# Row halves and paired chunks in one attention loop, moved pieces of work in another

## The reference

```python
xn = _ln(x, lnx_g, lnx_b)                                  # first layer
yn = _ln(y, lny_g, lny_b)                                  # y: the context
q = jnp.einsum('bsc,hcd->bhsd', xn, wq)
k = jnp.einsum('btc,hcd->bhtd', yn, wk)
v = jnp.einsum('btc,hcd->bhtd', yn, wv)
a = jax.nn.softmax(jnp.einsum('bhsd,bhtd->bhst', q, k) * D ** (-0.5), axis=-1)
o = jnp.einsum('bhst,bhtd->bhsd', a, v)
```

## Time and profile before

| | |
|---|---|
| median of 3 runs | 628.16 us (627.39 to 629.56) |
| profiled execution | 629.66 us, span 627.8 us |
| mean granted PE clock | 0.98 of 2.4 GHz |
| first loop, first scores of images 0 to 3 and last scores | 115.9, 140.71, 165.45, 189.98; 304.3 us |
| second loop, the same | 411.06, 441.28, 463.97, 486.66; 589.0 us |
| busy share of the span | PE 90%, DVE 71%, POOL 61%, ACT 59% |

### The profile page before, as it was taken

The page is one execution under the profiler, slowest core; times in us unless marked ns, Lnnn a source line. Parts: engine busy times, 40 slices in busy tenths (PEclk is TensorE's granted clock), DMA queues, the critical chain, the costliest instruction groups (busy, mean ns, idle before and its releaser), DMA issues.

```text
span 627.8 us, 18969 instructions
## 1 busy us (share of the span) xinstructions
PE 566.9 (90%) x8256; PEld 416.1 (66%) x8256; DVE 444.7 (71%) x698; ACT 372.0 (59%) x623; POOL 380.6 (61%) x271
## 2 busy tenths in 40 slices
PE   9788898899999999999888979977889889889897
PEld 4566775566767767666777556664667767778765
DVE  3876728697887887786356774776888988986543
ACT  2335674657657667566462417474677777777552
POOL 1572451488989889864630231175999999977500
PEclk9789999999999999999999999997999999999998
DMA  5830015002101101010013000412422432330000
GB/s 169 238 133 2 3 40 180 2 1 42 34 7 41 26 15 40 3 40 3 2 60 123 2 0 3 99 39 64 103 67 45 96 78 52 78 77 4 2 1 15
DMA packets 33838, 31.81 MB, mean 51 GB/s; under 512 B 27124, under 2 KB 27380, under 8 KB 33756
## 3 DMA queue, kind: packets, MB, share of 16 engines
q1 hardware_dynamic: 33756, 30.60, 18.8%
HBM read 13.06 MB, written 0.23 MB: 21 GB/s over the span
## 4 chain that ended last, share of the span: by engine, by line
PE 62%; DVE 18%; ACT 8%; issue 7%; POOL 3%; DMA 1%; DVEq 0%; POOLq 0%; ACTq 0%
PE psum L1143 9%; DVE scratch L1306 6%; PE psum L1067 5%; PE psum L1119 5%; PE psum L1503 4%; PE psum L1112 4%; PE psum L1114 4%; PE psum L1526 4%; DVE scratch L1291 4%; PE psum L217 3%; POOL scratch L1291 2%; ACT scratch L1276 2%; POOL scratch L652 1%; PE psum L1073 1%; PE psum L248 1%
## 5 line engine op out<-in xcount | busy, mean ns | idle before, releaser
L1291 POOL TENSOR_TENSOR scratch<-scratch 125x896 bf16<-125x896 f32 x143 | 242.7, 1715 | 80.4 <-ACT scratch L1276 79.9
L1306 DVE TENSOR_REDUCE scratch<-psum 128x1 f32<-128x500 f32 x336 | 210.3, 672 | 23.1 <-PE psum L1067 9.6
L1276 ACT ACTIVATE scratch<-psum 125x896 f32<-125x896 f32 x192 | 173.6, 917 | 82.8 <-PE psum L1143 51.1
L1112 PE MATMUL psum<-tok_high,scratch 125*128 125x65 bf16 x1344 | 107.0, 194 | 3.3 <-issue 2.7
L1114 PE MATMUL psum<-tok,scratch 125*128 125x64 bf16 x1344 | 106.4, 194 | 0.0
L1112 PEld LDWEIGHTS psum<-tok_high,scratch 125*128 125x128 bf16 x1344 | 94.8, 98 | 13.9 <-ACT scratch L1276 6.0
L1114 PEld LDWEIGHTS psum<-tok,scratch 125*128 125x128 bf16 x1344 | 88.6, 98 | 17.1 <-issue 0.5
L1143 PE MATMUL psum<-scratch 65*128 65x448 bf16 (+1 forms) x384 | 87.3, 352 | 0.0
L1291 DVE TENSOR_TENSOR scratch<-scratch 125x896 bf16<-125x896 f32 x49 | 67.5, 1383 | 22.8 <-ACT scratch L1276 21.1
L1119 PE MATMUL psum<-tok_high,scratch 125*128 125x65 bf16 x1344 | 72.7, 194 | 4.8 <-POOL scratch L1291 3.1
L1503 PE MATMUL psum<-scratch 128*128 128x500 bf16 x168 | 64.2, 382 | 10.8 <-DVE scratch L1306 6.5
(11 more groups left out here) (340 smaller groups left out, 870.5 us busy)
## 6 DMA issues: line engine op xcount, KB each, us to landing
nrm<-scratch SPq DMA_DIRECT2D x64, 96.0 KB, 2.2
nrm<-w_third SPq DMA_DIRECT2D x32, 96.0 KB, 2.2
raw<-ctx_dram SPq DMA_DIRECT2D x4, 672.0 KB
w_third<-fifth_dram SPq DMA_DIRECT2D x3, 595.0 KB, 6.0
w_third<-third_dram SPq DMA_DIRECT2D x2, 844.0 KB, 8.9
w_third<-third_dram SPq DMA_DIRECT2D x2, 843.5 KB, 6.8
w_fourth<-fourth_dram SPq DMA_DIRECT2D x3, 542.5 KB, 5.8
scratch<-scratch SPq DMA_DIRECT2D x8, 192.0 KB, 2.6
```

Of the source, the lines that this page charges most:

```text
L1112: nc.tensor.matmul(psum[:, sums, 65 * r:65 * r + 65], rows, t1[:, c, :], start=(c == 0 and r == 0), stop=False, skip_group_check=True)
L1276: nc.scalar.activation(CR["p"][0:CP, n % RING, :].rearrange("p (f n) -> p f n", f=2), psum[0:CP, S:S + 2, 0:HALF], ACT.Exp).then_inc(self. ...
L1291: ops.tensor_tensor(CR["pl"][0:CP, n % RING, :], CR["p"][0:CP, n % RING, :], p_high(n % RING), ALU.subtract).then_inc(done, 1)
L1306: nc.vector.tensor_reduce(mxp[:, r, t:t + 1], bank(B, TB), X_AXIS, ALU.max).then_inc(self.aux_freed, 1)
```

## The change

First loop. The scores of an even chunk and of the next are issued together: the four `ya` matmuls of both, then the four `yb` matmuls. `yb` and `qb` now keep one copy on each 64-row half of the array: a row of ones or shifts first, then 63 rows. This takes away the row for feature 0: since normalized tokens sum to zero over their features, the weights of feature 0 are subtracted from all others once (`fold_keys_pool`). The `yb` matmul of column half 0 runs on rows 0 to 63, that of half 1 on rows 64 to 127. Ones are set in four places, `yb` is copied in twice (63 rows each), the two shift units cover 448 columns each, and ACT's shift copy waits for DVE's low queries, which write the same row earlier. M units move to chunks 3 to 9, O to chunk 6, N between the maxima of chunk 3.

Second loop. M units are at new places, DVE's low parts in chunks 3 and 4 (were 1 and 2; in the first image they stay), key units in chunks 0 and 1 of the first image and 9 and 10 of every image (were 0 to 2, and 8 to 10), the masked queries in chunk 5 (was 10). The tokens' casts move from POOL to ACT in chunk 2, and POOL's low tokens to chunk 3, for images 3 to 7. The first copy for `pv` (`high_act`) of image 1 moves two steps down. Image 2's transpose is issued ahead of image 1's grouping.

```diff
@@ ONES moves up; new:
+        def fold_keys_pool(pool):
+            keys = par("a2_wk").rearrange("p (h d) -> p h d", d=65)
+            nc.gpsimd.tensor_copy(keys[:, :, 64:65], keys[:, :, 0:1]).then_inc(key_scaled, 1)
+            pool.wait_ge(key_scaled, 2)
+            nc.gpsimd.tensor_tensor(keys[:, :, 0:64], keys[:, :, 0:64], keys[:, :, 64:65].to_broadcast([128, HEADS, CD]),
+                                    ALU.subtract).then_inc(key_scaled, 1)
+            pool.wait_ge(key_scaled, 3)
@@ y_ones_set
-                nc.gpsimd.memset(CR["yb", i][64:65, :], 1.0).then_inc(y_ones, 1)
+                for k in range(2):
+                    nc.gpsimd.memset(CR["yb", i][64 * k:64 * k + 1, :].bitcast(F32), ONES).then_inc(y_ones, 1)
@@ placement
-                for c in range(4, 11):
-                    at[c] += [[u] for u in FRONT[3 * c - 10:3 * c - 7]]
+                for c in range(3, 10):
+                    at[c] += [[u] for u in FRONT[3 * c - 7:3 * c - 4]]
...
-                at[3] += [[], [("N", 0)]]
-                at[5] += [[("O", 0)]]
+                at[3] += [[] for _ in range(1 - len(at[3]))]
+                at[3].insert(1, [("N", 0)])
+                at[6].insert(0, [("O", 0)])
@@ Cross.scores_pe
-                for lhs, rhs, rows in ((CR["ya", i], CR["qa", i], 128), (CR["yb", i], CR["qb", i], 65)):
-                    if c == 0 and rows != 128:
-                        self.wait_freed(pe, self.index("A", 1, b))
-                        pe.wait_ge(self.yb_in, 16 * (b + 1))
+                if n % 2:
+                    return
...
+                for m in (n, n + 1):
+                    if m >= 2:
+                        pe.wait_ge(self.probs, m - 1)
+                    for f in range(2):
+                        nc.tensor.matmul(bank(2 + 2 * (m % 2) + f, HALF), CR["ya", i][:, chunk(m)],
+                                         CR["qa", i][:, HALF * f:HALF * f + HALF], start=True, stop=False,
+                                         skip_group_check=True)
+                if n % CHUNKS == 0:
+                    self.wait_freed(pe, self.index("A", 1, b))
+                    pe.wait_ge(self.yb_in, 32 * (b + 1))
+                    pe.wait_ge(self.front_low, 2)
+                for m in (n, n + 1):
+                    for f in range(2):
+                        rows = slice(64 * f, 64 * f + 64)
+                        mm = nc.tensor.matmul(bank(2 + 2 * (m % 2) + f, HALF), CR["yb", i][rows, chunk(m)],
+                                              CR["qb", i][rows, HALF * f:HALF * f + HALF], start=False, stop=True,
+                                              skip_group_check=True)
+                        if f:
+                            mm.then_inc(self.scores, 1)
@@ copy_act, shift row
+                    if b and self is cross1:
+                        self.wait_freed(act, self.index("Q", 1, b))
+                    lo, hi = HALF * k, HALF * k + HALF
@@ Cross.turn_tokens
-                sp.dma_start(CR["yb", b % 2][0:64, :], CR["ya", b % 2][64:128, :]).then_inc(self.yb_in, 16)
+                if b:
+                    sp.wait_ge(self.yb_in, 32 * b)
+                for k in range(2):
+                    sp.dma_start(CR["yb", b % 2][64 * k + 1:64 * k + 64, :], CR["ya", b % 2][65:128, :]
+                                 ).then_inc(self.yb_in, 16)
@@ new: tokens' casts on ACT
+            def high_tokens(self, act, b, k):
+                at = slice(CHUNKS * b + 6 * k, CHUNKS * b + 6 * k + 6)
+                act.wait_ge(self.pv_done, CHUNKS * (b - 2))
...
+                nc.scalar.activation(tok[b % TOKENS][:, 6 * k:6 * k + 6, 64:128], self.src[:, at, :], ACT.Copy
+                                     ).then_inc(self.tok_high, 1)
@@ KeyCross: maxima per chunk, key units, low parts, POOL
-                    for c, n in enumerate((2, 1, 1, 2, 3, 3, 3, 2, 2, 1, 1) if b else (0, 0, 0, 0, 3, 3, 3, 3, 3, 3, 3)):
+                    for c, n in enumerate((2, 1, 3, 1, 0, 2, 3, 3, 3, 2, 1) if b else (0, 0, 1, 3, 3, 3, 3, 2, 2, 2, 2)):
...
-                    if b == 0 and c < 3:
-                        lots += [[], [], [("K", c)]]
+                    if b == 0 and c < 2:
+                        lots += [[("K", 0)], [("K", 1)]] if c == 0 else [[("K", 2)]]
...
-                    if b < BATCH - 2 and 8 <= c < 11:
-                        lots += [[]] * (2 - len(lots)) + [[("K", c - 8)]]
+                    if b < BATCH - 2 and c in (9, 10):
+                        lots += [[]] * (2 - len(lots)) + ([[("K", 0)]] if c == 9 else [[("K", 1)], [("K", 2)]])
...
+            def tokens_pool(self, pool, b, c):
+                if b == 0 and c in (1, 2):
+                    self.split_tokens(pool, 2, c - 1)
+                if b and c == 3:
+                    for k in range(2):
+                        self.low_tokens(pool, b + 2, k)
...
             def beside_act(self, act, b, c):
+                if b and c == 2 and b < BATCH - 2:
+                    for k in range(2):
+                        self.high_tokens(act, b + 2, k)
...
             def beside_dve(self, dve, b, c):
-                if c == 10 and b < BATCH - 2:
+                if c == 5 and b < BATCH - 2:
                     self.plain_dve(dve, b + 2)
@@ the sync queue in the second loop
             for b in range(BATCH):
+                if b == 1:
+                    cross2.turn_tokens(sp, 2)
                 cross2.group_keys(sp, b)
-                if 0 < b < BATCH - 1:
+                if 1 < b < BATCH - 1:
                     cross2.turn_tokens(sp, b + 1)
```

More of the change, by code:

```diff
@@ L1071, in pe_unit @@
                         pe.wait_ge(self.max_set, b + 1)
-                    for r in range(4 * k, min(4 * k + 4, ROWT)):
-                        mm = nc.tensor.matmul(psum[:, B, 128 * (r % 4):128 * (r % 4) + 128],
-                                              nmx[:, r:r + 1].to_broadcast([128, 128]), ident16[:, :],
-                                              start=True, stop=True)
+                    for r in range(3 * k, 3 * k + 4):
+                        lo, hi = max(128 * r, HALF * k), min(128 * r + 128, HALF * k + HALF)
+                        mm = nc.tensor.matmul(psum[:, B, lo - HALF * k:hi - HALF * k],
+                                              nmx[:, r:r + 1].to_broadcast([128, 128]),
+                                              ident16[:, lo - 128 * r:hi - 128 * r], start=True, stop=True)
                 elif kind == "N":
@@ L1133, in scores_pe @@
             def scores_pe(self, pe, n):
-                b, c, i = n // CHUNKS, n % CHUNKS, n // CHUNKS % 2
-                S = 2 + 2 * (n % 2)
-                for lhs, rhs, rows in ((CR["ya", i], CR["qa", i], 128), (CR["yb", i], CR["qb", i], 65)):
-                    if c == 0 and rows != 128:
-                        self.wait_freed(pe, self.index("A", 1, b))
-                        pe.wait_ge(self.yb_in, 16 * (b + 1))
-                        pe.wait_ge(self.front_low, 2)
-                    for f in range(2):
-                        mm = nc.tensor.matmul(bank(S + f, HALF), lhs[0:rows, 128 * c:128 * c + 128],
-                                              rhs[0:rows, HALF * f:HALF * f + HALF],
-                                              start=(rows == 128), stop=(rows != 128), skip_group_check=True)
-                return mm
+                if n % 2:
+                    return
+                b, i = n // CHUNKS, n // CHUNKS % 2
+                chunk = lambda m: slice(128 * (m % CHUNKS), 128 * (m % CHUNKS) + 128)
+                if n == 0:
+                    self.wait_freed(pe, self.index("A", 1, 0))
+                for m in (n, n + 1):
+                    if m >= 2:
+                        pe.wait_ge(self.probs, m - 1)
+                    for f in range(2):
+                        nc.tensor.matmul(bank(2 + 2 * (m % 2) + f, HALF), CR["ya", i][:, chunk(m)],
[13 more added lines that the diff above has]
+                            mm.then_inc(self.scores, 1)
             def run_pe(self, pe, start, projection=None):
@@ L1423, in plan @@
             def plan(self):
-                return [("K", k) for k in range(3)] + FRONT[2:], (1, 2), (1, 2)
+                return [("K", k) for k in range(3)] + FRONT[2:], (3, 4)
             def place(self, b):
```

79 lines of the change are left out of this document (47 added, 32 removed).

## The result

The changed kernel takes 639.33 us (median of 4, 635.16 to 642.24) beside 628.86 us (627.39 to 632.31) for the kernel before on the same chip: a ratio of 1.0143, 95% interval 1.0098 to 1.0188. It is slower; the forecast was 618.4 us. The profiled execution took 638.12 us, its span 636.3.

The account below looks back on a forecast made before the run. PE was taken to pace the first loop's middle images, DVE most of its first image, waits the second loop's middle images. +0.6 and -10.4 us sum to -9.8: 619.9 us profiled, 618.4 by the median; range 610 to 626.

Parts of the forecast that it names:

- Halves overlap: First loop, line 1143: two 64-row halves run together, so a pair of chunks costs 1.32 us instead of 1.52.
- A: Rival, first loop: mode changes hidden in a dense stream, each pair saves 0.19 us more; 612.9 us; chance 0.18.
- D: Rival, first loop: halves run serially and each change between them costs a hand-over; 637.6 us; chance 0.07 with serial form.
- The wait ahead of chunk 3's maxima: First loop, middle image: PE waits 1.7 us for the turned tokens, whose transpose lands at X+10.65.
- X: Start of the pair of chunks 10 and 11 in a first-loop middle image, from which the walk counts microseconds.
- the tail of the walk: First loop, middle image, X+10.65 to X+24.7: sums, maxima, pairs and projection on PE, with DVE's reductions keeping up.
- the gain is eaten, +0.1 on each of six images: First loop: PE's work falls to 23.0 us, the 1.7 us wait cancels the saving; period 24.53 before, 24.6 after.
- First image -6.6: Second loop: earlier transpose closes PE's idle hole and half clock; next scores at 434.65 instead of 441.28; bounds -3, -8.
- No clock of 0.5: Sign for the second loop: once the hole at 426 to 430 us closes, no stretch at the 1.2 GHz level.
- rival B: Second loop: the hole only moves, DVE's low-key buffer waits for copies, half clock stays; gives 3.5, 625.3 us; chance 0.12.
- to 17.6: Second loop, images 1 to 5: twelve maxima and masked queries end 17.6 us in; image 22.0 us, -0.7 each.
- rival C: Second loop: full DVE/POOL port lock, chunk 4's low part waits up to 1.64 us; 3.5 us worse, 621.9; chance 0.08.

Follow-up runs that it names:

- The table of four: First-loop periods, units at old places: whole rows by the chunk (kernel before) 24.52 us, in pairs 25.87; halves by the chunk 24.69, in pairs 24.94.
- SP's order alone: Kernel before, only image 2's transposes issued ahead of image 1's key copies in the second loop: 627.45 us, ratio 0.995.
- both places repaired: Changed kernel with the first loop's units in their old chunks and the second loop's masked-query product back in chunk 10: 625.26 against 631.87 us, ratio 0.9897.
- without pairs and halves: Kernel before with only the second loop changed, its masked-query product left in chunk 10: 620.55 against 630.22 us, ratio 0.9854.

## Why the prediction was wrong

**First loop, +0.6 forecast, some +11 us measured.**
- Halves overlap, 0.09 us at each hand-over, 1.32 us a pair: right (1.33 from 189.59 to 190.92). PE's busy time fell 1.0 us an image between pairs of whole rows and pairs of halves (24.45 to 23.43); 6 x 0.19 = 1.14 was forecast. Rivals A and D fall.
- The wait ahead of chunk 3's maxima, 1.7 us from X+8.9 to X+10.65: right in place and releaser, 1.39 us idle, about 1.55 counted by starts of matmuls, up to X+10.94 (X = 189.59). I overlooked that chunk 10's low part stands behind chunk 9's on POOL, so that the sums of chunk 10 wait (0.4 to 0.5 us); the next pair, forecast at X+3.67, came at X+4.22.
- The step that failed is the tail of the walk: from the first maximum to the next image 14.05 us in the forecast, 14.8 measured, and with it "the gain is eaten, +0.1 on each of six images". I let DVE keep up, since six reductions fit in a pair's time. They come late or in bursts, and PE's weight loads wait for them, two times, 1.1 us in all, beside PE's matmuls:

```profile
PEld psum L1081 <- DVE scratch L1335: 1.1, 2, 0.6
```

The first is behind DVE's low parts: the one at 196.82 started 0.14 us after POOL's and took 2.48 us, and the reductions begin at 201.62, 1.1 us after the first maximum's matmul. The second is in the burst of six that follows the pair at X+16.93. Each time the matmuls come 0.3 us late. Walking PE alone hid that pairing itself leaves 1.3 us more of PE unused an image. I had costed the pairing only as hand-overs saved. The table of four gives +1.35 us for pairing whole rows and -0.93 for the halves within pairs; the places add 0.77. Together +1.19 us an image, where I had +0.1. The range missed for these terms, not for the size of the saving.
- The period of image 5, +3.6 us: a transpose of 5.15 us, and a clock of 0.72 from 252 to 258 behind the wait. I took 3.69 from one row as if it held for every image. The long one in the trace before was covered by the 1.8 us ahead of the maxima, and moving the maxima forward used that up. It is no accident of one trace: in 14 of the 16 traces one of the first loop's last two transposes (of six) takes 4.3 to 5.4 us, and the three kernels with the early maxima of the changed kernel and its order of POOL have 27.65 to 28.13 us in image 5.
- First image +0.9, measured +2.25: 1.1 of it is the early places (25.92 without). Last image -0.9, measured -0.93: right.

**Second loop, -10.4 forecast, -3.5 measured.**
- First image -6.6, measured -4.55, and -3.8 by SP's order alone, inside my bounds of -3 and -8. The transpose left 6.4 us into the loop as forecast and the hole closed. What I had not seen: with key units ahead of them, DVE's two low parts (chunks 1 and 2) come late, and PE twice waits 0.95 us; behind these waits the clock still falls to the 1.2 GHz level (0.55 from 430.6 to 434.0). "No clock of 0.5" was wrong for this trace; this is rival B's sign with another cause, and that the loop gives the 3.5 us of rival B is chance. The fall does not come every time: of the six traces with this second loop unaltered, three show it (clock 0.93 over the image, 25.65 to 25.74 us), and three have the same two waits without it (1.00, 24.38 to 25.16 us). So the moves and waits alone leave the first image 5.1 to 5.8 us shorter, and the clock decides the rest.
- Images 1 to 5: -0.7 each, measured +0.31. The step that failed is one line, the masked queries "to 17.6": I gave the product 0.7 us where it stood, and it took 1.79. With it in chunk 10 the period is 22.06, the 22.0 of the forecast. So this one operation carries what the walk missed (that the other steps are right is not tested one by one), and it was the full hold of rival C, which I had weighed for low parts only: I priced it at 3.5 us, and five images of 0.94 make 4.7. The Trainium skill, SBUF — State Buffer, Who interferes with whom, says that a DVE instruction with two SBUF inputs contends with a GpSimd instruction that reads SBUF, and that the second to come is blocked for the whole of the first. The rows at 475.63 and 481.07 agree: 0.62 us ahead of POOL's, 1.79 us during it. The hold should have gone into the sum for each operation of DVE whose two inputs are in SBUF.
- Image 6 -0.95 (forecast -0.8), last image +0.44 (+0.5): right.

With both places repaired the change gives 0.9897, -6.5 us; without pairs and halves 0.9854. Pairs and halves don't pay in any image with maxima (0.17 to 1.35 us lost); in the last image, without maxima, both together save 1.05 us. What stays open is why some transposes take up to 5.4 us, and what would remove the unused PE time in pairs: the list of waits above puts 1.0 us of it behind maxima and 0.5 behind an exponential, but no run takes one of them away.

## What to carry to other kernels

When a bound engine's work is regrouped, price the grouping itself: run it once without the saving it is meant for. Here pairs of whole rows cost 1.35 us an image and the halves inside them gave back 0.93. Moving a consumer earlier spends the slack that covered its producer's worst case, so look for the longest transfer, not the median. Before moving an operation of DVE with all operands in SBUF, look at what POOL does there and at what is queued behind it; its duration in the old place says nothing of the new one. And where whole runs of one kernel differ by a per cent, compare the stretch that the change touches.

## What the runs showed of the hardware

- DVE's product of two SBUF tiles, 128 x 896 in bf16: 0.62 us when it starts just ahead of POOL's subtraction, 0.79, 1.46 and 1.79 us when it starts during one, each time ending 0.48 us after POOL's end (the 0.79 with the place of the kernel before, the 1.46 with low parts back in 1 and 2). DVE's low part likewise: 1.08 us free, otherwise nearly always to 0.95 us past POOL's end. POOL's next subtraction takes 2.05 instead of 1.68 us when it starts inside one of DVE's.
- Two 64-row halves started 0.003 to 0.004 us apart and each two of them 0.2 us behind the last; 0.09 us to change over, at 448 columns as at 56.
- The same transpose of tokens took 3.7 to 3.9 us in the first images of the first loop (4.3 once) and up to 5.4 us in one of the last two: 5.42 us at 265.64 in the kernel before and 5.15 us at 248.17 in the changed kernel, with no other transfer of the program under way. The same was seen in 14 of 16 traces.
- When PE had idled for a transpose (changed kernel, 2.84 us up to 253.39), the granted clock went to the 1.2 GHz level for 3.4 us (0.72 as the mean of 252 to 258). After the same two waits of 0.9 us at the second loop's start it fell in three traces of six.
